# Split products in three passes with the late low part last, new orders on all engines, and three weight splits moved off GpSimd

## The reference

```
x = x + L0(x)      L0: 16-head attention with a key mask (k, q, v, o of 256 x 256), RMS norm of its result,
                   times (1 + scale) and plus shift, both from silu(cond) @ Wc.T + bc
x = x + L1(x)      L1(x) = y + swiglu(norm(y)), y = x + attention(norm(x)), no mask, hidden width 1024
                   norm(x) = g * x * rsqrt(mean(x*x) + eps) + b, with g and b linear in cond
```

## Time and profile before

| | |
|---|---|
| median of 3 runs | 324.95 us (324.79 to 325.38) |
| profiled execution, its own time | 326.49 us |
| its span, first to last instruction | 324.7 us |
| mean granted TensorE clock | 0.995 of full speed |
| TensorE busy | 315.1 us, 97% of the span |
| VectorE, ScalarE, GpSimd busy | 238.2, 204.5, 181.4 us |

### The profile page before, as it was taken

The page is one execution under the profiler, slowest core; times in us unless marked ns, Lnnn a source line. Parts: engine busy times, 40 slices in busy tenths (PEclk is TensorE's granted clock), DMA queues, the critical chain, the costliest instruction groups (busy, mean ns, idle before and its releaser), DMA issues.

```text
span 324.7 us, 11938 instructions
## 1 busy us (share of the span) xinstructions
PE 315.1 (97%) x5016; PEld 297.6 (92%) x5016; DVE 238.2 (73%) x425; ACT 204.5 (63%) x445; POOL 181.4 (56%) x207
## 2 busy tenths in 40 slices
PE   7989999999989999999999999999999999999996
PEld 6869878899989999999999999998999999999995
DVE  4796769896997898796959598798963783554344
ACT  3787587989884577588475765685572466333231
POOL 7296798334767376468651766479280653553310
PEclk9997999999999999999999999999999999999999
DMA  7955841304000300300003000100000100000010
GB/s 228 302 151 138 249 150 34 101 2 134 2 3 2 99 2 2 101 35 2 4 0 102 32 6 0 36 0 5 0 3 2 35 32 2 2 10 25 2 34 33
DMA packets 11238, 17.08 MB, mean 53 GB/s; under 512 B 1328, under 2 KB 5440, under 8 KB 11184
## 3 DMA queue, kind: packets, MB, share of 16 engines
q1 hardware_dynamic: 11008, 15.80, 16.0%
q0 software_dynamic: 176, 0.51, 0.7%
HBM read 14.14 MB, written 2.16 MB: 50 GB/s over the span
## 4 chain that ended last, share of the span: by engine, by line
PE 80%; DVE 6%; POOL 4%; DMA 3%; issue 3%; ACT 2%; DVEq 0%; POOLq 0%; ACTq 0%
PE ps L1589 62%; PE ps L1712 5%; PE ps L1694 5%; DMA w_stage<-in_weights 3%; PE ps L1745 3%; DVE row_max L1140 2%; PE ps L1777 2%; DVE probs L1148 2%; PE ps L1730 1%; PE ps L1682 1%; POOL w_lo L411 1%; POOL x_row L422 1%; PE ps L1756 1%; ACT probs_T L713 1%; DVE mod_tile L1183 0%
## 5 line engine op out<-in xcount | busy, mean ns | idle before, releaser
L1589 PE MATMUL ps<-ff_hi,w_hi 128*128 128x256 f32 x256 | 72.9, 285 | 0.9 <-DVE ff_lo L1221 0.9
L1589 PE MATMUL ps<-ff_lo,w_hi 128*128 128x256 f32 x256 | 72.1, 282 | 0.0
L1589 PE MATMUL ps<-ff_hi,w_lo 128*128 128x256 f32 x256 | 72.1, 281 | 0.0
L474 POOL TENSOR_TENSOR h_lo<-w_stage,h_hi 128x512 fp32r<-128x512 f32 x29 | 37.4, 1291 | 43.6 <-ACT h_hi L769 43.6
L468 POOL TENSOR_TENSOR probs<-probs,inv_row 128x512 f32<-128x512 f32 x40 | 41.3, 1051 | 34.2 <-DVE inv_row L1161 34.2
L1589 PEld LDWEIGHTS ps<-ff_hi,w_hi 128*128 128x128 f32 x256 | 48.2, 188 | 1.5 <-issue 1.0
L1140 DVE TENSOR_REDUCE row_max<-ps 128x8 f32<-128x512 f32 x64 | 40.8, 680 | 10.6 <-PE ps L1694 10.4
L1589 PEld LDWEIGHTS ps<-ff_hi,w_lo 128*128 128x128 f32 x256 | 48.2, 188 | 0.0
L1589 PEld LDWEIGHTS ps<-ff_lo,w_hi 128*128 128x128 f32 x256 | 48.2, 188 | 0.0
L706 ACT ACTIVATE probs<-probs 128x512 f32<-128x512 f32 x64 | 38.8, 634 | 11.2 <-DVE probs L1148 10.9
L1234 DVE SCALAR_TENSOR_TENSOR w_stage<-w_stage,ps 128x512 f32<-128x512 f32 x32 | 21.7, 677 | 30.4 <-ACT w_stage L762 30.3
(11 more groups left out here) (111 smaller groups left out, 825.2 us busy)
## 6 DMA issues: line engine op xcount, KB each, us to landing
w_stage<-in_weights SPq DMA_DIRECT2D x20, 256.0 KB, 4.7
mod_tile<-mod_rows_dram SPq DMA_DIRECT2D x32, 128.0 KB, 3.2
x_T<-in_xT SPq DMA_DIRECT2D x8, 256.0 KB, 3.3
x_row<-in_x SPq DMA_DIRECT2D x8, 256.0 KB, 2.8
out<-x SPq DMA_DIRECT2D x7, 256.0 KB, 2.1
x<-in_cond POOLq DMA_DIRECT2D x1, 392.0 KB, 6.5
out<-x SPq DMA_DIRECT2D x2, 128.0 KB, 1.9
x<-in_rows POOLq DMA_DIRECT2D x1, 96.0 KB, 6.3
```

Source lines behind the costliest of these rows:

```text
L474: pool.tensor_tensor(h_lo[q % 2][:], h_T[q % 2], h_hi[q % 2][:], ALU.subtract)\
L1589: mm = pe.matmul(dst, x, y, start=first and n == 0, stop=last and n == len(terms) - 1, skip_group_check=True)
```

## The change

split_product is replaced by products(blocks, part), which does one of the three kinds for all halves of a call: first high times high, then the low part that is there early, then the one that comes late, with the waits set between the passes. keys, values and hidden_in take the late part second or first according to the side on which it stands; first_keys goes. The high parts of k1 and q1 are made by ScalarE and the low part of v1 by VectorE (HI_POOL = 6, LO_DVE = 7). All lists of calls and all PSUM bank tables are new; the calls in them are the same except for these splits. The core of the diff (the rest of the lists is of the same kind):

```diff
     'g2': 10, 'g3': 11, 'h0': 12, 'h1': 13, 'h2': 14, 'h3': 15, 'u0': 16, 'u1': 17, 'u2': 18,
     'u3': 19,
 }
-LO_DVE, HI_POOL, NSTAGE = 6, 4, 5
+LO_DVE, HI_POOL, NSTAGE = 7, 6, 5
 
 
 
@@ -56,32 +56,32 @@
...
+            load_xT(0)
             load_w("k0")
-            load_xT(0)
             load_w("q0")
             load_w("v0")
+            load_xT(1)
             load_w("o0")
             load_w("k1")
-            load_xT(1)
+            load_xT(2)
             load_w("q1")
-            load_xT(2)
             load_w("v1")
             load_w("o1")
+            load_xT(3)
             load_w("g0")
             load_w("g2")
-            load_xT(3)
+            load_xT(4)
+            store_mods()
+            load_rows(0)
             load_w("h0")
             load_w("h2")
-            load_xT(4)
+            load_xT(5)
+            load_rows(1)
             load_w("u0")
             load_w("u1")
             load_w("g1")
-            store_mods()
+            load_rows(2)
             load_w("g3")
-            load_xT(5)
-            load_rows(0)
-            load_rows(1)
             load_w("h1")
             load_w("h3")
+            load_xT(6)
             load_w("u2")
             load_w("u3")
-            load_rows(2)
-            load_xT(6)
             load_rows(3)
             load_rows(4)
             load_xT(7)
...
 
             set_up_ident()
+            load_mask()
             set_up_values(0)
-            load_mask()
             set_up_values(1)
             load_consts()
-            weight_hi("k1")
-            weight_hi("q1")
             weight_hi("v1")
-            weight_lo("v1")
             weight_hi("o1")
             weight_lo("o1")
             weight_hi("g0")
+            weight_lo("g0")
             weight_hi("g2")
-            weight_lo("g0")
+            weight_lo("g2")
+            root_of_y(0)
+            shift_row(0)
             weight_hi("h0")
-            weight_lo("g2")
+            new_x1(0)
+            weight_hi("h2")
             weight_lo("h0")
-            weight_hi("h2")
+            root_of_x(0)
+            weight_lo("h2")
+            shift_row(1)
             weight_hi("u0")
             weight_hi("u1")
-            weight_lo("h2")
+            bias_in(0)
             weight_hi("g1")
-            weight_hi("g3")
             weight_lo("u0")
             weight_lo("u1")
+            root_of_y(1)
             weight_lo("g1")
+            new_x1(1)
+            weight_hi("g3")
+            weight_hi("h1")
             weight_lo("g3")
-            root_of_y(0)
-            shift_row(0)
-            new_x1(0)
-            shift_row(1)
-            weight_hi("h1")
-            root_of_x(0)
+            weight_lo("h1")
             weight_hi("h3")
             weight_hi("u2")
+            weight_lo("h3")
+            weight_lo("u2")
             weight_hi("u3")
-            weight_lo("h1")
-            bias_in(0)
-            weight_lo("h3")
+            root_of_x(1)
+            weight_lo("u3")
             shift_row(2)
-            weight_lo("u2")
-            root_of_y(1)
-            weight_lo("u3")
-            new_x1(1)
-            root_of_x(1)
             shift_row(3)
+            bias_in(1)
             root_of_y(2)
-            bias_in(1)
             new_x1(2)
             clear_sums(6)
+            root_of_y(3)
             root_of_x(2)
...
             weight_hi("q0")
             weight_hi("v0")
             copy_keys(0)
+            input_hi(1)
             weight_hi("o0")
+            weight_hi("k1")
             copy_queries(0)
-            input_hi(1)
             copy_values(0)
+            copy_keys(1)
             input_hi(2)
-            copy_keys(1)
+            weight_hi("q1")
             copy_queries(1)
+            condition()
             exponentials(0, 0)
-            condition()
             copy_values(1)
+            input_hi(3)
             exponentials(0, 1)
-            copy_keys(2)
             exponentials(0, 2)
             exponentials(0, 3)
             copy_pT(0, 0, 0)
-            input_hi(3)
+            copy_pT(0, 0, 1)
             exponentials(1, 0)
-            copy_pT(0, 0, 1)
             copy_pT(0, 1, 0)
             copy_pT(0, 1, 1)
             exponentials(1, 1)
...
             dve.memset(probs[0][:], 0.0).then_inc(warm_set, 1)
             set_up_parity()
+            input_lo(0)
             weight_hi("k0")
             weight_lo("k0")
-            input_lo(0)
+            set_up_mask()
             weight_lo("q0")
             weight_lo("v0")
-            set_up_mask()
+            input_lo(1)
             weight_lo("o0")
             weight_lo("k1")
-            input_lo(1)
-            weight_lo("q1")
             maximum(0, 0)
             maximum(0, 1)
             maximum(0, 2)
+            shift(0, 0)
+            shift(0, 1)
+            condition()
             maximum(0, 3)
-            shift(0, 0)
+            shift(0, 2)
+            shift(0, 3)
             input_lo(2)
-            shift(0, 1)
-            shift(0, 2)
-            condition()
-            shift(0, 3)
             maximum(1, 0)
             maximum(1, 1)
             shift(1, 0)
+            shift(1, 1)
+            mod_rows_in()
             maximum(1, 2)
             maximum(1, 3)
-            shift(1, 1)
-            mod_rows_in()
             shift(1, 2)
+            modT_in()
...
                     pe.wait_ge(s, count)
 
-            def split_product(dst, pairs, first=True, last=True):
-                terms = [(x[i], y[j]) for x, y in pairs for i, j in ((0, 0), (0, 1), (1, 0))]
-                for n, (x, y) in enumerate(terms):
-                    mm = pe.matmul(dst, x, y, start=first and n == 0, stop=last and n == len(terms) - 1,
-                                   skip_group_check=True)
+
+
+            BOTH_HIGH, SECOND_LOW, FIRST_LOW = (0, 0), (0, 1), (1, 0)
+
+            def products(blocks, part, closing=False):
+
+                for dst, pairs, opens in blocks:
+                    for n, (x, y) in enumerate(pairs):
+                        mm = pe.matmul(dst, x[part[0]], y[part[1]], start=opens and part == BOTH_HIGH and n == 0,
+                                       stop=closing and n == len(pairs) - 1, skip_group_check=True)
                 return mm
+
+            def weight_hi(name):
...
-            def project_features(a, name, bank):
-                for m in range(KT):
-                    mm = split_product(ps[:, bank, TC * m:TC * m + TC],
-                                       [(w_parts(name, k, P * m, P), (in_hi[a % NS][:, k, :], in_lo[a % NS][:, k, :]))
-                                        for k in range(KT)], first=m == 0)
-                return mm
+            def features(a, name, bank):
+                return [(ps[:, bank, TC * m:TC * m + TC],
+                         [(w_parts(name, k, P * m, P), (in_hi[a % NS][:, k, :], in_lo[a % NS][:, k, :])) for k in range(KT)],
+                         m == 0) for m in range(KT)]
 
             def keys(a, *readers):
                 c, l = CHAINS[a]
+                blocks = features(a, f"k{l}", K_BANK[a])
+                if c == 0:
+                    pe.wait_ge(*weight_hi(f"k{l}"))
+                pe.wait_ge(in_hi_ready, a + 1)
+                bank_free(*readers)
+                products(blocks, BOTH_HIGH)
                 if c == 0:
                     pe.wait_ge(*weight(f"k{l}"))
+                products(blocks, FIRST_LOW)
                 pe.wait_ge(in_lo_ready, a + 1)
-                bank_free(*readers)
-                project_features(a, f"k{l}", K_BANK[a]).then_inc(k_ready, 1)
-
-            def first_keys():
...
+                products(blocks, SECOND_LOW, closing=True).then_inc(k_ready, 1)
...
             def output_product(a, *readers):
                 c, l = CHAINS[a]
+                blocks = [(ps[:, Y_BANK[a], D * t:D * t + D],
+                           [((o_hi[a % 2][:, t, k, :], o_lo[a % 2][:, t, k, :]), w_parts(f"o{l}", k, 0, D)) for k in range(KT)],
+                           t == 0) for t in range(NT)]
+                if c == 0:
+                    pe.wait_ge(*weight_hi(f"o{l}"))
+                pe.wait_ge(o_hi_ready, a + 1)
+                bank_free(*readers)
+                products(blocks, BOTH_HIGH)
                 if c == 0:
                     pe.wait_ge(*weight(f"o{l}"))
+                products(blocks, SECOND_LOW)
                 pe.wait_ge(o_lo_ready, a + 1)
-                bank_free(*readers)
-                for t in range(NT):
-                    mm = split_product(ps[:, Y_BANK[a], D * t:D * t + D],
-                                       [((o_hi[a % 2][:, t, k, :], o_lo[a % 2][:, t, k, :]), w_parts(f"o{l}", k, 0, D))
-                                        for k in range(KT)], first=t == 0)
-                mm.then_inc(y_ready, 1)
+                products(blocks, FIRST_LOW, closing=True).then_inc(y_ready, 1)
...
             def hidden_out(k, j, *readers):
                 q = 4 * k + j // 2
```

(66 more changed lines are left out.)

1082 lines of the change are left out of this document (539 added, 543 removed), and 20 rows, old and new, of tables (GU_BANK, S_BANK, T_BANK).

## The result

The changed kernel took 330.03 us (median of 4 runs, 328.73 to 330.99) against 324.87 (4 runs, 324.78 to 325.38) for the kernel before: ratio 1.0145, 95% interval 1.0114 to 1.0176. Forecast were 321.7 us and "faster" with a chance of 0.71; the range ended at 326.0. The profiled execution took 329.53 us, span 327.7.

A forecast was written before the change was run, and what follows sets the result against it. TensorE was taken as the bound, with its idle time, overlaps and clock fall left to gain. Terms -1.5, -0.4, -1.0, +0.2, -0.2 and -0.4 sum to -3.3 us, forecasting 321.7 us against the median of 324.95; range 318.8 to 326.0.

The forecast's parts named there:

- The form, -1.5: Products in three passes: later waits for low parts remove the stops for ff_lo and o_lo, pitch unchanged; -1.5 us.
- Rival 5: In the products, passes lose a hidden weight load, 188 instead of 119 ns each: 132 us more, 454; chance 0.01.
- The start, -0.4: Stops ahead of weigh_values(0, 0) shrink from 2.6 to 1.7 to 2.4 us; gain 0.2 to 0.9, taken as 0.4.
- The stop for w_lo in queries(0): After two passes of queries(0), at 8.3 us, TensorE waits 0.9 to 1.6 us for q0's low part.
- The clock, -1.0: The fall of TensorE's granted clock from 26 to 30 us goes, as feature and row modulation are separated; -1.0 us.
- fall of the clock elsewhere: Listed sign that the forecast is wrong: TensorE's granted clock falls at another place; no size given.
- The new stop at transpose_normed(1), +0.2: TensorE arrives at 64.9 us, norm_x(1) ends at 65.1, behind root_x(1) and nine splits on GpSimd; +0.2 us.
- Rival 4: Slower by GpSimd's queue: nine splits ahead of root_x(1) make it late and TensorE waits; 326.0 us, chance 0.17.
- The middle, -0.2: From 35 to 97 us, six or so small stops go with their places and others come; -0.2 us.
- the late part, -0.4: From 97 us, h's low part is covered but hidden_out is drawn closer to hidden_in; -0.4 us.

The follow-up runs named there:

- e1: Kernel before with only the new form of the products, orders, banks, loads and weight split as before: 323.37 us, ratio 0.9934.
- e10: Kernel before plus four stretches of unread TensorE work behind its last product, one execution: 3.67 us per 256 instructions in the first, 4.19 with transfers in the fourth.
- bf16 runs: Transposed probabilities and values held as bf16: changed kernel 322.98 us, kernel before 324.75, kernel before with the new form of the products 322.36.
- e5: Changed kernel with queries(3) moved ahead of weigh_values(1, 0) and hidden_out(0, 1) ahead of weigh_values_T(6): 330.37 us, ratio 1.0141.
- e3: Changed kernel with load_rows(1) and all loads behind it held until weigh_values(1) is done: 328.39 us, ratio 1.0102.
- e7: Kernel before with 128 more TensorE instructions in its warm-up: 335.59 us, ratio 1.0308.
- e8: Changed kernel with the edits of both e5 and e6: 330.60 us, ratio 1.0169.
- e6: Changed kernel with three more waits on the load-issuing engine, holding bulk loads until output_product(0), weigh_values(1) or weigh_values(3): 331.44 us, ratio 1.0189.

## Why the prediction was wrong, step by step

- *The form, -1.5.* Right in mechanism and size: e1 gives -1.5 to -2.1, the waits for ff_lo, o_lo and w_lo are gone, and the products keep their pitch of 0.119 us. Rival 5, a lost weight load, is out.
- *The start, -0.4.* Right in direction, mis-sized: weigh_values(0, 0) starts at 24.04 instead of 26.14, 2.1 sooner. But most of this is the execution that the forecast was counted on: in e10 the kernel before, unchanged, starts it at 24.31, with no wait of 1.2 us for in_lo, and e1, with the old orders, at 24.08. So the new start is worth some 0.3 us, and next to the form nothing that shows. The profile of before was a long one, 326.49 us against a median of 324.95. The stop for w_lo in queries(0), forecast at 0.9 to 1.6, is not there. The mask took 4.3 us, not the 6.0 of the earlier trace rows, and was turned at 5.96; w_lo of q0 began at 7.07, ahead of the third pass. A transfer's duration in one execution is no constant, and neither is a wait.
- *The clock, -1.0.* It stays at 1.00 from 5 to 35 us, as forecast; then it falls at 39 us behind the stop of 2.3 us, for 1.5. The "fall of the clock elsewhere" was on the list of what would show me wrong.
- *The new stop at transpose_normed(1), +0.2.* 0.52 at 68.44 us. The mean and the root behind the nine splits ended at 64.45, forecast 64.5. What came later than forecast is norm_x(1): VectorE began it at 66.21, behind o_row, for whose product (weigh_values, with the stop at packet 8 in it) it had waited 3.02 us, and needed 2.17 us where 0.6 had been put. Rival 4, which had the sign, had the wrong mechanism: GpSimd's queue was not late.
- *The middle, -0.2, and the late part, -0.4.* Here the prediction failed. Of the 6.30 us of idle time from 35 to 97, 3.7 are the stops at packets 3, 7 and 8; the other 2.6 are what it was before, 2.50. Of the 1.13 behind 97, 0.53 is packet 15; the other 0.60 is what it was before, 0.66, so the -0.4 isn't there either.

The step that failed is "TensorE is the bound, and the question is what is left of its idle time", with the sum built on data waits only: a stage may run as soon as its operands are there. The sum lacks a term for TensorE's own instructions: 5.1 us of stops and 1.5 of clock. 329.53 - 5.06 - 1.5 = 323.0 us is what remains (counted from one trace, not measured). The forecast, by the same profiled execution, was 326.49 - 3.3 = 323.2. That the two agree is in part luck, for the 326.49 was long by itself. e1 took 323.37 with a fall of the clock still in it (0.94 from 5 to 35 us), so the new orders, even without the stops, gained nothing beyond the form, which the bf16 runs show by another way. The row that could have warned me stood on the page: 40 instruction packets, and weigh_values at 128 matmuls in 1.44 us. The kernel before had the same dense stages. That none of its boundaries fell badly is chance as far as its trace tells: in e10 the same program has one stop of 0.45 us, at 80.3 us, and 64 or 128 instructions of warm-up undo it altogether.

Open is what fixes the moment at which a packet starts. With no transfer in the way it started mostly some 1 us behind the instruction about 300 ahead of the boundary, yet in e5 the late packet began at 53.35 us, 7 us behind it, with idle DMA engines for about half of that time. Many late starts lie 1.0 us behind the end of a semaphore wait of TensorE's; whether that is the cause was not tried. So the share of the bulk transfers in the lateness of packets 3 and 8 isn't settled either: they ran (DMA share 1.06 above), e3 changed little by holding part of them back, and e10 puts their mean cost at 0.5 us.

## What to carry to other kernels

Count instructions, not only time: where more than about 256 instructions of TensorE run in less than 3.7 us, check against the instruction queue's packets whether they can be there. A stop inside a run of equal instructions, or one whose named releaser was long done, is the sign. Before two orders of such a kernel are compared, compare them at several alignments (a few dozen instructions added to the warm-up do it), for the alignment alone was worth up to 10 us here, more than the change. Of this change the part worth keeping is the form of the products: 323.37 us, 0.7% faster than the kernel before, with no late packet.

## What the runs showed of the hardware

- TensorE's program comes in 16 KB packets of 256 instructions while it runs. All 70 stops found (of over 0.35 us, in twelve kernels) stand at record 256 n + 449, and end 1.16 to 1.68 us behind the end of packet n. The packet itself takes 0.9 to 1.4 us in the changed kernel.
- Back to back, a packet comes every 3.67 us (3.58 where products lie between, 4.19 beside bulk transfers); small matmuls of 34 columns in fp32, four instructions each, use one up in 1.3.
- 128 instructions that delay the first product by 0.3 us made the kernel before 3.1% slower.
- The profile names a stop for instructions "issue" inside a stage, and after any semaphore the next instruction has at the head of one (1.66 us "for in_lo" in e7).
- A stop of 2.3 us was followed by a fall of the granted clock, 1.5 us dearer for 24 products; one of 0.36 us at the same place was not. A longer stop need not bring one: behind the stop of 2.8 us in weigh_values(2) the clock fell in e5 and e8 and stayed at 1.00 in e6.
- The same program begins its products at full pace or at half of it: four took 0.85 us up to 9.5 us in e3, 0.45 from some 7.6 us on in the changed kernel, with 1.00 given as the granted clock in both.
